# Row scores of an attention block in two-bank pairs under one maximum, column scores in two banks instead of three

## What is computed

```python
h = _layernorm(x, axis=-1) * (1 + ca) + sa
qkv = jnp.einsum('bnc,ce->bne', x, w_qkv)
attn = jnp.einsum('bhnd,bhmd->bhnm', q, k) / scale
attn = jax.nn.softmax(attn, axis=-1)
out = jnp.einsum('bhnm,bhmd->bhnd', attn, v)
x = x + ga * _L0_attn_ref(h, L0_attn_w_qkv, L0_attn_w_out)
h = _layernorm(x, axis=-1) * (1 + cb) + sb
x = x + gb * _L0_ffn_ref(h, L0_ffn_w_router, L0_ffn_w_gate, L0_ffn_w_up, L0_ffn_w_down)
```

## Time and profile before

| quantity | value |
|---|---|
| median of 3 runs | 685.91 us (685.17 to 688.14) |
| span of the profiled execution, first to last instruction | 679.4 us |
| median less that span | 6.5 us |
| attention, batches after the first rows | about 52 to 464 us |
| experts | about 464 to 679 us |

### The profile page before, as it was taken

The page is one execution under the profiler, slowest core; times in us unless marked ns, Lnnn a source line. Parts: engine busy times, 40 slices in busy tenths (PEclk is TensorE's granted clock), DMA queues, the critical chain, the costliest instruction groups (busy, mean ns, idle before and its releaser), DMA issues.

```text
span 679.4 us, 13009 instructions
## 1 busy us (share of the span) xinstructions
PE 618.9 (91%) x3413; PEld 285.7 (42%) x3413; DVE 550.1 (81%) x1065; ACT 450.5 (66%) x859; POOL 267.2 (39%) x384
## 2 busy tenths in 40 slices
PE   5299999999999999999999999889899999999995
PEld 3112223323323322322322322225667777777773
DVE  3698889899888988988988988714788888888885
ACT  2107878778778778778778777876554555555553
POOL 4522022222222222222122122333567776776773
PEclk9658999999999999999999999979899999999999
DMA  7703505304304304303403400253334454345411
GB/s 183 197 31 82 183 3 117 106 20 106 117 19 95 126 17 95 127 17 79 143 18 72 150 18 4 76 167 109 92 114 139 137 142 141 130 137 150 136 35 31
DMA packets 48972, 65.58 MB, mean 97 GB/s; under 512 B 9432, under 2 KB 30432, under 8 KB 48928
## 3 DMA queue, kind: packets, MB, share of 16 engines
q1 hardware_dynamic: 46304, 64.32, 33.1%
q10 hardware_dynamic: 2624, 0.79, 0.5%
HBM read 47.26 MB, written 17.83 MB: 96 GB/s over the span
## 4 chain that ended last, share of the span: by engine, by line
PE 34%; DVE 20%; issue 19%; POOL 16%; ACT 5%; DMA 2%; SPq 1%; DVEq 1%; POOLq 0%; ACTq 0%
POOL hid_lo L612 13%; DVE negmax L864 13%; PE o_acc L1172 11%; PE s_row L1149 10%; PE s_col L1162 5%; ACT probs L656 3%; DVE probs L1042 1%; POOL h_lo L618 1%; PE misc L1130 1%; PE misc L1103 1%; PE misc L1100 1%; SPq L325 1%; DVE sums_inv L883 1%; DVE k_rest L878 1%; PE misc L1126 1%
## 5 line engine op out<-in xcount | busy, mean ns | idle before, releaser
L864 DVE TENSOR_REDUCE negmax<-s_row 128x1 f32<-128x512 f32 x512 | 323.0, 683 | 47.5 <-PE s_row L1149 41.9
L656 ACT ACTIVATE probs<-s_col 128x512 f32<-128x512 f32 x512 | 270.8, 599 | 76.4 <-PE s_col L1162 73.4
L1149 PE MATMUL s_row<-k_stack,q_stack 64*128 64x512 bf16 x512 | 141.7, 402 | 25.2 <-DMA k_stack<-k_scr 11.6
L612 POOL TENSOR_TENSOR hid_lo<-probs,hid_hi 128x512 fp32r<-128x512 f32 x87 | 128.5, 1493 | 61.9 <-ACT hid_hi L800 61.9
L1162 PE MATMUL s_col<-q_stack,k_stack 64*128 64x512 bf16 x512 | 132.4, 383 | 7.1 <-ACT probs L656 6.5
L1172 PE MATMUL o_acc<-probs,v_aug 128*32 128x512 f32 x1024 | 138.1, 612 | 0.0
L800 ACT ACTIVATE hid_hi<-probs 128x512 fp32r<-128x512 f32 x88 | 55.6, 632 | 85.0 <-DVE probs L1042 84.6
L1149 PEld LDWEIGHTS s_row<-k_stack,q_stack 64*128 64x128 bf16 x512 | 34.9, 93 | 180.1 <-DVE negmax L864 142.1
L1042 DVE TENSOR_TENSOR probs<-probs,q_stack 128x512 f32<-128x512 f32 x56 | 62.5, 1116 | 15.7 <-POOL hid_lo L612 13.6
L520 POOL CAST negmax_parts<-negmax 128x16 bf16<-128x16 f32 x32 | 6.3, 196 | 163.0 <-DVE negmax L864 163.0
L1032 DVE TENSOR_TENSOR probs<-probs,s_col 128x512 f32<-128x512 f32 x88 | 59.6, 677 | 2.9 <-ACT probs L820 1.6
(11 more groups left out here) (134 smaller groups left out, 713.9 us busy)
## 6 DMA issues: line engine op xcount, KB each, us to landing
q_scr<-q_parts SPq DMA_DIRECT2D x48, 128.0 KB, 2.4
k_scr<-k_parts SPq DMA_DIRECT2D x48, 128.0 KB, 2.4
q_stack<-q_scr SPq DMA_DIRECT2D x8, 768.0 KB, 6.1
k_stack<-k_scr SPq DMA_DIRECT2D x8, 768.0 KB, 7.5
q_stack<-combT_scr SPq DMA_DIRECT2D x24, 256.0 KB, 3.4
k_stack<-combT_scr SPq DMA_DIRECT2D x16, 224.0 KB, 2.9
q_stack<-combT_scr SPq DMA_DIRECT2D x16, 192.0 KB, 2.7
q_stack<-combT_scr SPq DMA_DIRECT2D x16, 160.0 KB, 2.6
```

Of the source, the lines that this page charges most:

```text
L612: nc.gpsimd.tensor_tensor(hid_lo[k % HIDDEN][:], weighed[(par + k) % 2], hid_hi[k % HIDDEN][:], ALU.subtract).then_inc(s["hid_split"], 1)
L656: nc.scalar.activation(probs[t % 2][:, j, :], s_col[score_bank("col", u)][:], ACT.Exp, scale=INV_SCALE).then_inc(s["exp_done"], 1)
L864: nc.vector.tensor_reduce(negmax[n % 2][:, j, qc:qc + 1], s_row[score_bank("row", u)][:], AX.X, ALU.max, negate=True).then_inc(s["row_max" ...
L1149: nc.tensor.matmul(s_row[score_bank("row", u)][:], q_stack[par][at:at + KS, head // 2, P * qc:P * (qc + 1)], k_stack[par][at:at + KS, head ...
```

## The change

The row banks become two tensors of two banks each. PE fills both banks of a pair (heads 2*half and 2*half+1), and only the second matmul signals. DVE takes one maximum over the 128 x 2 x 512 block, which gives 128 x 2 values; there are 256 such instructions instead of 512. The column banks fall from three to two, so that the eight banks still suffice, and a column matmul now waits for the exponential two units back. The jump in the rotation is gone.

```diff
-        s_row = [bank(f"s_row{i}") for i in range(SCORES)]
-        s_col = [bank(f"s_col{i}") for i in range(SCORES)]
+        s_row = [ctx.enter_context(nc.psum_tensor(f"s_row{i}", [P, 2, N], F32)) for i in range(2)]
+        s_col = [bank(f"s_col{i}") for i in range(COLS)]
...
-                nc.vector.tensor_reduce(negmax[n % 2][:, j, qc:qc + 1], s_row[score_bank("row", u)][:], AX.X, ALU.max,
+                nc.vector.tensor_reduce(negmax[n % 2][:, 2 * half:2 * half + 2, qc], s_row[pair % 2][:], AX.X, ALU.max,
                                         negate=True).then_inc(s["row_max"], 1)
...
-            REST = {(1, 2): "q", (2, 2): "k"}
+            REST = {(1, 1): "q", (2, 1): "k"}
...
+                if not (isinstance(b, int) and b == 0 and pair < 2):
+                    pe.wait_ge(s["row_max"], ROW_PAIRS * b + pair - 1)
+                for i in range(2):
+                    head = G * n + 2 * half + i
+                    at = 64 * (head % 2)
+                    last = nc.tensor.matmul(s_row[pair % 2][:, i, :], q_stack[par][at:at + KS, head // 2, P * qc:P * (qc + 1)],
+                                            k_stack[par][at:at + KS, head // 2, :], start=True, stop=True)
+                last.then_inc(s["row_ready"], 1)
...
-                    pe.wait_ge(s["exp_done"], UNITS * b + u + 1 - score_distance("col", u))
+                    pe.wait_ge(s["exp_done"], UNITS * b + u + 1 - COLS)
...
-                        for j in range(2 * half, 2 * half + 2):
-                            scores(j)
-                            col_scores(b, par, t, j)
+                        for j in range(2 * half, 2 * half + 2):
+                            col_scores(b, par, t, j)
```

More of the change, by code:

```diff
@@ L110, in adaln_block @@
     UNITS = SLOTS * G
[L114 to L122, removed]
+    ROW_PAIRS = SLOTS * 2
+    COLS = 2
     EXPERT_ROWS = [[(e, max(0, e * HID - P * k), min(P, (e + 1) * HID - P * k))
@@ L258, in k_bank @@
         def k_bank(b):
-            return s_row[SCORES - 1][:] if isinstance(b, int) and b == 0 else misc_f
-        g_ps, u_ps = ([a[:], b[:]] for a, b in (s_row[0:2], s_col[0:2]))
+            return s_row[1][:, 1, :] if isinstance(b, int) and b == 0 else misc_f
+        g_ps = [s_row[0][:, i, :] for i in range(2)]
+        u_ps = [a[:] for a in s_col]
         y_ps = o_acc[:]
-        ga_banks = [s_col[0], s_col[2]]
+        ga_banks = s_col
         names = """
@@ L973, in _ @@
             for t in range(AHEAD):
[L974 to L978 removed]
+                for half in range(2):
+                    row_max(0, 0, t, half)
+            REST = {(1, 1): "q", (2, 1): "k"}
             LN2_STATS = [(6, 1), (7, 0), (7, 1), (8, 0), (8, 1)]
@@ L984, in body @@
                     for half in range(3):
-                        for j in range(2 * half, 2 * half + 2) if half < 2 else ():
+                        at = (t, half)
+                        if half < 2:
                             if t < SLOTS - AHEAD:
-                                row_max(b, par, t + AHEAD, j)
+                                row_max(b, par, t + AHEAD, half)
                             elif not last:
[L989 to L992, removed]
+                                row_max(b + 1, 1 - par, t + AHEAD - SLOTS, half)
+                        if at in REST and not last:
+                            evacuate(None, b + 1, 1 - par, REST[at])
                         if not first:
@@ L1135, in task, with row_scores @@
                 last.then_inc(s["misc_full"], 1)
-            def row_scores(b, par, t, j):
+            def row_scores(b, par, t, half):
                 n, qc = t // CH, t % CH
[L1140 to L1143, removed]
+                pair = 2 * t + half
+                if t == 0 and half == 0:
                     pe.wait_ge(s["stacked_first"], 16 * LOADS * (b + 1))
-                if t == CH and j == 0:
+                if t == CH and half == 0:
                     pe.wait_ge(s["stacked"], 16 * LOADS * (b + 1))
[L1147 to L1150, removed]
+                if not (isinstance(b, int) and b == 0 and pair < 2):
[6 more added lines that the diff above has]
+                last.then_inc(s["row_ready"], 1)
             def col_scores(b, par, t, j):
```

34 lines of the change are left out of this document (16 added, 18 removed).

## The result

The changed kernel takes 725.63 us (median, 724.07 to 730.28), against 685.72 us before: 1.0598 times as long, 95% interval 1.0554 to 1.0643. The forecast was 723, range 711 to 737. The ratio on record leaves out executions that took over 1.5% more than the fastest of their kernel and is not the quotient of the two medians (1.0582 here); in the experiments the two differ by up to 0.7%, and nothing is read from differences as small as that.

A forecast was written before the change was run, and what follows sets the result against it. No engine is full; bank handovers among PE, DVE and ACT set the pace. First rows -1, two tasks ahead +0.5, first batch +6, middle +27.6, last +4.9: +38 on 679.4, span 717; with 6.5 to the median, 723 us, range 711 to 737.

The forecast's parts named there:

- the term that carries it: Plain tasks (no other job on PE): column score 3 waits for exponential 1, so 2.70 becomes 3.16 us.
- what hides: PE's new wait in each task: a half 0 job up to about 1.1 us costs nothing; later jobs add 3.5 us.
- Jobs of half 0: PE jobs such as `q`, `k`, `v`, `o0`, `proj`: covered by the new wait if up to about 1.1 us.
- jobs of half 1 and half 2: PE's `o1`, `x1T`, `attnT`, `router` and four `max` transposes: added in full, 3.5 us a middle batch.
- the turn of the loop: Middle batches: +0.6 us each, from five batches of 52.0 against one of 51.5, rounded up.
- The first rows: Stretch from 32.4 to 51.5, DVE always busy: 16 pairs save 0.07 each, about -1 us.
- the remainders: `q_rest` and `k_rest` on DVE, now behind four maxima, delay exponential 0: 0.7 us a batch, between 0 and 1.3.
- rival 3: Clock falls for 6.9 us in each of seven batches as PE rests longer: some +3 each, 744 us; 6%.
- the bridge from span to median: Whole kernel: 6.5 us added to the forecast span of 717 to give the median, 723 us.
- six middle batches: Each goes from 51.9 to 56.5 us, +4.6; six together +27.6.
- The lower bound: If remainders and late exponentials cost nothing, a middle batch gains 3.3 at least: sum 27, 712 us.
- The 0.55 from matmul to exponential: Last batch without row scores: exponential 0 starts 0.55 after its matmul; used for the 0.05 release and the 1.69 task.

The follow-up runs named there:

- Half exponentials: The changed kernel with exponentials of only the first 256 of 512 columns: 678.74 us, ratio 0.9876 to the kernel before.
- the single missing column bank: The kernel before with two column banks instead of three, three single row banks and the old order on PE: 719.75 us, ratio 1.0493.
- the mirrored split: The kernel before with two banks for rows and four for columns: 741.92 us, ratio 1.0828.
- early remainders: The changed kernel with the remainders of q and k taken between the two maxima of their task instead of behind both: 714.62 us, ratio 1.0474.
- work for PE: The changed kernel with the second row-score pair computed three times in tasks without a PE job at half 0: 718.47 us, ratio 1.0512.
- jobs of half 1 in pairs: The changed kernel with early remainders, and PE's jobs of half 1 except task 5's put ahead of column score 2: 701.46 us, ratio 1.0291.

## Why the prediction was right, point by point

**Right: the term that carries it.** A plain task was to go from 2.70 to 3.16 and went to 3.17, by the chain that was worked out (exponential 0 at T+0.72, column score 3 at T+1.86, weighing at T+2.17). Half exponentials, the single missing column bank and the mirrored split all gave the plain tasks that the same arithmetic gives: 2.74, 3.17 and 3.30. In the first and last batch, whose code is written out rather than looped, it is 3.09, since there the first exponential starts at T+0.64. The last batch's plain tasks without rows took 2.88 at full clock (expected 2.39+0.49).

**Right: what hides.** Jobs of half 0 cost nothing (3.16 to 3.17 in tasks 3, 9 and 15), jobs of half 1 and half 2 are added in full (4.95 for task 11). The undisturbed middle batch is +3.9; the forecast had 4.6, of which 0.6 was the turn of the loop. The first rows: 16 pairs were to give 1 us and did, 18.20 us from the first maximum to the end of unit 32 against 19.23 before.

**Mis-sized: the remainders.** The remainder of q delays task 2 by 0.57 (3.73 against 3.17), that of k delays nothing (task 3 takes 3.17): 0.57 in place of 0.7, right by its sum more than by its parts. The remainder of k did come late, but the longer task 2 gave DVE the time back. This is also why the pair is no gain: its 0.06 a pair (1.14 from one maximum to the next against twice 0.60) matters only in the first rows.

**Wrong: the clock.** This was rival 3 with 6%, on the ground that the trace had a fall only behind a stretch in which PE was busy for 2.02 of 3.4 us, while a plain task would keep it at work for about 2.1 of 3.16. It now fell behind 2.54 of 3.40, and a plain task keeps PE busy for 2.55 of 3.17 (before, 2.57 of 2.71). In the profile the five falls cost 6.9 us in the middle batches (1.3 where one falls into task 12), and the last batch, with 17 us at half clock, took 2 us more than forecast. The step that failed is to have judged the clock by PE's busy share in one old stretch: stretches with 2.31 and 2.32 of 3.40 pass without a fall, so the share does not decide. What does is open.

**Wrong: the bridge from span to median.** The 6.5 us between span and median were carried over as if they lay around the span. The changed kernel's profiled execution has both numbers, 728.5 and 730.28: only 1.8 lie around it. The profiled execution of before was thus about 4.5 below its median, and that of after 4.7 above. Span by span the ledger is:

| part | forecast | measured |
|---|---|---|
| up to the first weighing | -0.5 | +1.4 |
| first batch | +6 | +6.0 |
| six middle batches | +27.6 | +33.3 |
| last batch | +4.9 | +6.9 |
| experts | 0 | +1.5 |
| sum | +38 | +49.1 |

Of the 33.3, six times 3.9 are the order, 6.9 the clock, and about 2 a longer wait for the DMA of the maxima in task 6 of three batches. The +1.4 of the first line is not the pair's: its first maximum started 1.6 us later than before, and four profiles of kernels with the same first rows (half an exponential, early remainders, work for PE, jobs of half 1 in pairs) have the first weighing at 56.3 to 57.5 us, against 58.05 before and 59.49 here. From median to median it is +39.9, where +37 was forecast. The closeness of 723 to 725.6 is therefore partly luck: in the six middle batches the order costs 4.2 us less than forecast, and the falls of the clock, which had been left out, 6.9 more.

**Slips in the working.** The lower bound should say that a middle batch gains 2.8 at least (4.6 less 1.1 and 0.7), not 3.3; its sum of 27 goes with 2.8. The sum 679.4 + 38 + 6.5 is 723.9, not 723. The 0.55 from matmul to exponential is in the trace, but the earlier trace rows show 0.49. None of them moves the forecast by 1 us.

## What to carry to other kernels

When two producers share one in-order engine, count for each ring of buffers what stands behind the instruction that waits: with a distance of two the fourth score waited for a second, serial exponential, and a 1 us weighing and all of the next task's scores waited with it. A saving on an engine that is not full (DVE, 81%) buys next to nothing (1 us here) if it is paid for with a buffer of a chain that ends within 0.1 us of the path. Moving the weighing about in the loop removed the wait in none of three tries; a job whose input is ready can be hidden in it (the router: task 11 from 4.95 to 3.98).

## What the runs showed of the hardware

- One maximum over two banks took 1220 ns against 683 for one, and 1.14 us from one to the next against 0.60: the second bank costs only its values, 1.05 ns each.
- Where neither has to wait, row scores of an even and an odd head start within 0.01 us of each other and run side by side, whether they are issued next to each other or with a column score in between (the earlier trace rows and the plain task after). In the kernel before the second row score (174.52) thus starts 0.22 ahead of the column score that stands before it in the order on PE (174.74).
- The granted clock fell to 1.2 GHz although PE's longest rest in the stretch before was under 1 us: it had been busy for 2.54 of 3.40 us. It stayed at 2.4 GHz behind another stretch of the same kernel with 2.32 of 3.40 and a rest of 1.13. With four added matmuls in the wait of seven tasks of sixteen, the profile has no fall in the middle batches.
- A column score that waits only for its bank follows the end of the exponential that frees it by 0.05 to 0.06 us in nearly all cases. Where ACT is idle, an exponential follows the start of its matmul by 0.49 in the plain tasks of the changed kernel's loop and by 0.41 in those of its first batch, which is written out; 0.41 is seen in the loop as well, so the loop alone is not shown to be the reason.
